# ScalarE splits off the high part of h, the last batch's routing moves behind a layer, SyncE asks for rows ahead of weights

## The reference

```python
def ffn(x, ...):                      # 8 experts, each token uses 2
    logits = einsum('bsd,de->bse', x, gate_w) + gate_b
    probs = softmax(logits, axis=1)   # over the 256 tokens of a batch
    vals, idx = top_k(probs, 2)
    h = relu(einsum('bsd,edo->ebso', x, w1) + b1)
    h = relu(einsum('ebso,eop->ebsp', h, w2) + b2)
    y = relu(einsum('ebso,eop->ebsp', h, w3) + b3)
    onehot = one_hot(idx, E)
    w_tok = einsum('bske,bsk->bse', onehot, vals)
    ind = onehot.max(axis=2)
    v = einsum('ebso,bse->eo', y, w_tok)
    return einsum('bse,eo->bso', ind, v)

# x (16, 256, 512), ctx (16, 256, 512), all f32; attention without a mask, scale 1/sqrt(512)
x = x + tanh(g_xattn) * softmax(layernorm(x) @ Wq @ K.T * scale) @ V     # K, V = ctx @ Wkv
x = x + tanh(g_ffn) * ffn(layernorm(x), ...)
```

## Time and profile before

| | us |
|---|---|
| median of 3 runs | 954.37 |
| the three runs | 958.21, 954.37, 951.24 |
| the profiled execution, its own time | 953.95 |
| its span in the profile | 952.2 |
| mean granted clock of TensorE | 0.981 |

### The profile page before, as it was taken

The page is one execution under the profiler, slowest core; times in us unless marked ns, Lnnn a source line. Parts: engine busy times, 40 slices in busy tenths (PEclk is TensorE's granted clock), DMA queues, the critical chain, the costliest instruction groups (busy, mean ns, idle before and its releaser), DMA issues.

```text
span 952.2 us, 18810 instructions
## 1 busy us (share of the span) xinstructions
PE 918.2 (96%) x5746; PEld 863.7 (91%) x5746; DVE 721.6 (76%) x1379; ACT 419.5 (44%) x594; POOL 454.7 (48%) x402
## 2 busy tenths in 40 slices
PE   9999999999999979999999999999999999999985
PEld 6989888899888869899999999999999999999981
DVE  5667787887888867876877786889877777777646
ACT  5454443544433455344444444444444444444311
POOL 4225444444434566653655453655544554455213
PEclk9999999999999998999999999999999999999995
DMA  6433322233211544446656777866565555564008
GB/s 233 155 114 110 130 91 88 93 127 115 106 66 67 143 128 84 135 90 184 184 165 172 208 215 221 239 222 184 133 173 158 150 154 148 150 185 119 17 16 352
DMA packets 91924, 138.67 MB, mean 146 GB/s; under 512 B 28528, under 2 KB 56944, under 8 KB 88688
## 3 DMA queue, kind: packets, MB, share of 16 engines
q1 hardware_dynamic: 84464, 120.86, 42.8%
q0 software_dynamic: 7424, 17.38, 6.2%
HBM read 106.66 MB, written 31.53 MB: 145 GB/s over the span
## 4 chain that ended last, share of the span: by engine, by line
PE 65%; issue 11%; POOL 7%; DVE 6%; DMA 5%; SPq 4%; ACT 1%; POOLq 0%; DVEq 0%; ACTq 0%
PE bank L1319 20%; PE bank L1320 19%; PE bank L1321 19%; POOL h_lo L674 4%; POOL xg L664 3%; DMA rows_dram<-xg 2%; DMA xg<-xn_dram,idx 2%; DVE x_all L1309 2%; PE bank L1333 1%; PE bank L1390 1%; SPq L541 1%; PE bank L1431 1%; DMA idx<-slot_pair 1%; SPq L463 1%; PE bank L1433 1%
## 5 line engine op out<-in xcount | busy, mean ns | idle before, releaser
L674 POOL TENSOR_TENSOR h_lo<-h,h_hi 128x704 fp32r<-128x704 f32 x96 | 183.6, 1916 | 245.2 <-DVE h_hi L1190 245.2
L1319 PE MATMUL bank<-h_hi,w_hi 128*128 128x352 f32 x752 | 245.7, 327 | 7.3 <-POOL h_lo L674 4.1
L1321 PE MATMUL bank<-h_hi,w_lo 128*128 128x352 f32 x752 | 243.6, 324 | 0.0
L1320 PE MATMUL bank<-h_lo,w_hi 128*128 128x352 f32 x752 | 242.6, 323 | 0.0
L930 DVE TENSOR_TENSOR w_lo<-w_raw,w_hi 128x2048 fp32r<-128x2048 f32 x72 | 181.0, 2514 | 22.4 <-ACT w_hi L825 18.0
L836 ACT ACTIVATE h<-bank,bias 128x352 f32<-128x352 f32 x192 | 95.8, 551 | 201.0 <-PE bank L1321 170.8
L825 ACT ACTIVATE w_hi<-w_raw 128x2048 fp32r<-128x2048 f32 x72 | 137.8, 1916 | 54.6 <-PE bank L1321 46.0
L1319 PEld LDWEIGHTS bank<-h_hi,w_hi 128*128 128x128 f32 x752 | 142.1, 189 | 9.6 <-issue 9.6
L1320 PEld LDWEIGHTS bank<-h_lo,w_hi 128*128 128x128 f32 x752 | 142.1, 189 | 0.0
L1321 PEld LDWEIGHTS bank<-h_hi,w_lo 128*128 128x128 f32 x752 | 141.7, 188 | 0.0
L1319 PE MATMUL bank<-et_hi,w_hi 128*128 128x352 f32 x384 | 125.0, 326 | 4.5 <-DVE part L1226 2.6
(11 more groups left out here) (202 smaller groups left out, 1767.1 us busy)
## 6 DMA issues: line engine op xcount, KB each, us to landing
w_raw<-in_w SPq DMA_DIRECT2D x24, 1024.0 KB, 5.1
xq<-rows_dram SPq DMA_DIRECT2D x80, 176.0 KB, 4.1
w_raw<-in_w SPq DMA_DIRECT2D x48, 256.0 KB, 6.1
rows_dram<-xg SPq DMA_DIRECT2D x20, 512.0 KB, 3.1
wb<-slot_pair SPq DMA_DIRECT2D x24, 352.0 KB, 4.1
xt_raw<-in_x_t SPq DMA_DIRECT2D x16, 512.0 KB, 3.9
c_raw<-in_ctx_t SPq DMA_DIRECT2D x16, 512.0 KB, 3.3
x_all<-in_x SPq DMA_DIRECT2D x16, 512.0 KB, 4.8
```

The costliest lines, as they stand in the source:

```text
L674: pool.tensor_tensor(h_lo[n][:, 2 * k:2 * k + 2], h[:, 2 * k:2 * k + 2], h_hi[n][:, 2 * k:2 * k + 2].bitcast(F32), ALU.subtract).then_inc( ...
L1319: pe.matmul(out_ap, lh, rh, start=(i == 0), stop=False)
L1320: pe.matmul(out_ap, lh, rl, start=False, stop=False)
L1321: last = pe.matmul(out_ap, ll, rh, start=False, stop=(i == n - 1))
```

## The change

- ScalarE makes `h_hi`, directly behind each half of the relu; `h_high` is gone from VectorE.
- TensorE transposes all three chunks of tile 0 in one go, `p_times_v` of the last batch comes ahead of the gate logits of batch 14, and the ranks of batch 13 go into the middle of the last `values`. ScalarE and VectorE split tile 0's first weights between the second and the third chunk.
- Layer 2 of tile 0 begins on the first half of `h` (`layer2_first`), and the last batch's rows are transposed between its output halves; `slots` of the last batch is awaited by tile 1's layer 2 and no longer by tile 0's layer 3. Banks are dealt out anew for this.
- SyncE issues in its loop: store of the rows, `idx`, quarters, weights of layer 1, bias, `wb`. VectorE's two small steps on `wb` and bias (`weights_of`) move ahead of the weights' subtraction. `early_table` moves behind `exp_bias` of batch 14.

The diff, cut:

```diff
@@ layer_banks, row_banks, gate_banks
-            first = {(0, 0): (0, 1, 2, 3), (0, 1): (4, 5, 6, 2), (1, 0): (2, 3, 0, 1)}
+            first = {(0, 0): (0, 1, 2, 3), (0, 1): (4, 5, 6, 0), (1, 0): (0, 1, 2, 3),
+                     (2, 0): (4, 5, 6, 0), (1, 1): (1, 2, 3, 7)}
...
-            first = {0: (1, 2, 0), 1: (4, 5, 6), 2: (3, 0, 1)}
+            first = {0: (1, 2, 0), 1: (4, 5, 6), 2: (1, 2, 3)}
...
-            return [bank[0], bank[1]] if isinstance(m, int) and m == B - 1 else bG
+            return [bank[4], bank[5]] if isinstance(m, int) and m == B - 1 else bG
@@ SyncE, tile
+                if has_tile(3, left) and not isinstance(j, int):
+                    store_rows(j + 3)
+                if has_tile(4, left):
+                    load_idx(j + 4)
                 if has_tile(3, left):
+                    if not isinstance(j, int):
+                        load_quarters(j + 3)
                     load_w(0, j + 3)
-                    if not isinstance(j, int):
-                        store_rows(j + 3)
                 if has_tile(1, left):
                     load_b(2, j + 1)
                     load_wb(j + 1)
-                if has_tile(3, left) and not isinstance(j, int):
-                    load_quarters(j + 3)
-                if has_tile(4, left):
-                    load_idx(j + 4)
@@ ScalarE, relu_half
                     act.activation(h[:, oc], layer_banks(n, m)[oc][:, 0:TILE], ACT.Relu,
                                    bias=bias[n][:, oc:oc + 1]).then_inc(relu_done[n], 1)
+                need(act, l_done[n + 1], 2 * m)
+                if n == 1 and isinstance(m, int) and m == 0:
+                    act.wait_ge(gate_done, B)
+                act.wait_ge(relu_done[n], DC * m + 2 * k + 2)
+                act.activation(h_hi[n][:, 2 * k:2 * k + 2], h[:, 2 * k:2 * k + 2], ACT.Copy).then_inc(h_his[n], 1)
@@ ScalarE, the change of phases
-            et_high(0)
+            et_high(0, range(2))
             split_w(0, 0)
+            et_high(0, range(2, TH))
             gate_exp(B - 2)
             split_w(1, 0)
             act.wait_ge(b_in[0], 16)
             relu_half(0, 0, 0)
+            relu_half(0, 0, 1)
             norm2(B - 1)
-            relu_half(0, 0, 1)
             et_high(1)
+            split_w(0, 1)
             gt_high(B - 1)
-            split_w(0, 1)
             split_w(2, 0)
             relu(1, 0)
+            split_w(1, 1)
             gate_exp(B - 1)
-            split_w(1, 1)
@@ VectorE, batch
+                if isinstance(b, int) and b == KNOWN + 2:
+                    early_table()
...
-                if isinstance(b, int) and b == KNOWN + 1:
-                    early_table()
@@ VectorE, the change of phases
-            et_low(0)
+            et_low(0, range(2))
             w_low(0, 0)
+            et_low(0, range(2, TH))
             gate_softmax(B - 2)
             attended(B - 1)
             w_low(1, 0)
-            h_high(0, 0)
             two_best(B - 2)
             et_low(1)
-            gt_low(B - 1)
             slots(B - 2, (B - 2) % 2)
             w_low(0, 1)
+            gt_low(B - 1)
+            w_low(2, 0)
             gate_softmax(B - 1)
-            h_high(1, 0)
-            w_low(2, 0)
+            w_low(1, 1)
             two_best(B - 1)
-            h_high(0, 1)
-            w_low(1, 1)
-            slots(B - 1, (B - 1) % 2)
             w_low(0, 2)
             et_low(2)
+            slots(B - 1, (B - 1) % 2)
+            weights_of(0)
             weighted_sum(0)
@@ TensorE
+            def values_with_ranks(m, c, ranked):
...
+                for i in range(DC):
+                    if i == DC // 2:
+                        ranks(ranked)
...
+            def layer2_first():
+
+                need(pe, w_los[1], 1)
+                for k in range(2):
+                    need(pe, h_los[0], k + 1)
+                    for oc in range(2):
...
+                        for i in range(2 * k, 2 * k + 2):
...
+                last.then_inc(l_done[1], 1)
...
                 if isinstance(m, int) and m == 1:
                     need(pe, relu_done[0], 2 * DC)
+                    if k == 1:
+                        need(pe, slot_step, NSTEP * (B - 1) + 4)
                 layer_half(1, m, k)
...
-                if isinstance(m, int) and m == 0 and k == 1:
-                    need(pe, slot_step, NSTEP * (B - 1) + 4)
@@ TensorE, the change of phases
-            ranks(B - 3)
-            values(B - 1, 1)
+            values_with_ranks(B - 1, 1, B - 3)
             pt_transposes(B - 1)
             xn2_transposes(B - 2)
             need(pe, qa_los, 2 * B)
-            row_transposes(0, range(2))
+            row_transposes(0)
+            p_times_v(B - 1)
             gate_logits(B - 2)
-            row_transposes(0, range(2, TH))
-            p_times_v(B - 1)
             layer1_half(0, 0)
             gate_transposes(B - 2)
             layer1_half(0, 1)
             row_transposes(1)
+            layer2_first()
+            ranks(B - 2)
             xn2_transposes(B - 1)
-            ranks(B - 2)
-            layer2_half(0, 0)
+            layer2_half(0, 1)
             gate_logits(B - 1)
-            layer2_half(0, 1)
             layer1_half(1, 0)
+            layer1_half(1, 1)
             gate_transposes(B - 1)
-            layer1_half(1, 1)
```

More of the change, by code:

```diff
@@ L1182, in w_low @@
                 low(w_lo[n][:], w_raw[n][:], w_hi[n][:], w_los[n])
-            def h_high(n, m):
-                need(dve, l_done[n + 1], 2 * m)
-                if n == 1 and isinstance(m, int) and m == 0:
-                    dve.wait_ge(gate_done, B)
-                for k in range(2):
-                    dve.wait_ge(relu_done[n], DC * m + 2 * k + 2)
-                    dve.tensor_copy(h_hi[n][:, 2 * k:2 * k + 2], h[:, 2 * k:2 * k + 2]).then_inc(h_his[n], 1)
             def transpose_blocks(m):
@@ L1196, in transpose_blocks, with et_low @@
                               xq[:].rearrange("p g (i k) -> p g k i", k=DC)).then_inc(et_ready, 1)
-            def et_low(m):
+            def et_low(m, chunks=range(TH)):
                 if not isinstance(m, int):
@@ L1280, in tile @@
                         transpose_blocks(j + 2)
+                weights_of(j)
+                if has_tile(2, left):
                     w_low(0, j + 2)
                     et_low(j + 2)
-                if has_tile(0, left):
-                    weighted_sum(j, last=(left == 1))
+                weighted_sum(j, last=(left == 1))
             tiles = tiles_in_use(dve)
@@ L1493, in layer1_half @@
                     need(pe, part_done, m - 1)
+                    if isinstance(m, int) and m == 2 and k == 1:
+                        need(pe, relu_done[1], 2 * DC)
                 layer_half(0, m, k)
+            def layer2_first():
[3 more added lines that the diff above has]
+                    for oc in range(2):
+                        z = layer_banks(1, 0)[oc][:, 0:TILE]
+                        rows = slice(oc * P, (oc + 1) * P)
+                        for i in range(2 * k, 2 * k + 2):
+                            pe.matmul(z, w_hi[1][:, i, rows], h_hi[0][:, i], start=(i == 0), stop=False)
+                            pe.matmul(z, w_hi[1][:, i, rows], h_lo[0][:, i], start=False, stop=False)
+                            last = pe.matmul(z, w_lo[1][:, i, rows], h_hi[0][:, i], start=False, stop=(i == DC - 1))
+                last.then_inc(l_done[1], 1)
             def layer2_half(m, k, left=AHEAD + 1):
```

29 lines of the change are left out of this document (16 added, 13 removed).

## The result

The changed kernel takes 945.66 us, median of 20 runs (942.43 to 954.11), against 955.08 (951.24 to 958.21, 20 runs) of the kernel before on the same chip: ratio 0.9907, 95% interval 0.9890 to 0.9924. The gain is 0.93%, with an interval from 0.76 to 1.10% that doesn't reach zero; it falls just short of the 1% that the forecast took as what a measurement can tell. The profiled execution took 942.43 us, span 940.3: it is the quickest of the 20.

What follows compares the result with a forecast made beforehand. TensorE, 96% busy, was taken as the bound, with about 34 us of idle time and low clock to win. Change of phases 6.7 plus loop 4.7 less 0.1 made 11.3 us: 943 us forecast, range 938 to 952.

Steps and rivals of the forecast that it cites:

- rival (b): Loop's waits stay, by the lock of w_lo against h_lo and full DMA queues; gain only 6.6, 947.8 us; chance 0.18.
- Start of tile 0: Change of phases: earlier transposes and w_lo let layer 1 of tile 0 begin 2.4 us earlier, bounds 0 and 3.4.
- Layer 2 of tile 0: Change of phases: layer 2 begins 6.3 us earlier, behind one wait of 2 to 3 us for h_lo.
- Routing put off: Start of tile 1: slots and et_low(2) no longer hold TensorE; waits of 1.07 and 0.83 go, 1.9 us.
- The clock: Change of phases: one new low-clock stretch behind the 2.7 us idle time costs 2.3 us, ends 0 and 2.6.
- rival (a): Change of phases: no low-clock stretch at all, loop as forecast; 2.3 us less, 940.7 us; chance 0.22.
- The term of the change of phases: Gain up to the start of tile 1, 9.0 less 2.3 for the clock: 6.7 us, ends 3 and 9.5.
- `h_hi` on ScalarE: Moving 96 copies off VectorE costs nothing, covered by TensorE's other layer; only the last tile loses 0.1 us.
- The loop: SyncE's earlier idx and fewer VectorE copies leave 2.0 of 6.7 us of waits: gain 4.7 us.
- (d): Loop: SyncE becomes the bound, late weights delay h_lo and stall TensorE in ten tiles; about 967 us; chance 0.06.
- (c): First tile by blocks, tile 4: gain partly given back, about 3 us waited at layer 1; 950 us; chance 0.12.
- (e): Reordering does not reach TensorE: norm2 behind relus and copies delays the chain as much; 953 us; chance 0.08.

Runs made afterwards that it cites:

- runs 1 to 8: Two groups: one or two parts of the change without the rest; changed kernel with SyncE's order wholly or partly put back, or without layer 2's halves; ratios 0.9906 to 1.0166.
- u_sp: Changed kernel with SyncE's loop order put back to that of the kernel before: 942.33 us, ratio 0.9906 to the kernel before.
- runs 9 to 12: Changed kernel again; and with SyncE's old order, plain, with 14 filler matmuls, or with w_low(1, 0) behind two_best(14); ratios 0.9868 to 0.9920.
- v_sp: Changed kernel with SyncE's old loop order, measured once more beside the changed kernel on one chip: 944.13 us, ratio 0.9891 to the kernel before.
- v_after: The changed kernel once more, unaltered, as yardstick on another group's chip: 945.72 us, ratio 0.9920 to the kernel before.
- v_swap: Changed kernel with SyncE's old order and VectorE's w_low(1, 0) put behind two_best(14): 942.14 us, ratio 0.9868 to the kernel before.
- p_hi: Kernel before with only h_hi moved to ScalarE, all other orders as before: 946.14 us, ratio 0.9946 to the kernel before.
- p_phase: Changed kernel with VectorE making h_hi and SyncE's old loop order, so only the reordered change of phases stays: 950.23 us, ratio 0.9984 to the kernel before.
- u_hi: Changed kernel with VectorE making h_hi again, SyncE's new order kept: 954.82 us, ratio 1.0043 to the kernel before.
- p_sp: Kernel before with only SyncE's new loop order, VectorE unchanged: 959.65 us, ratio 1.0087 to the kernel before.
- u_idxlast: Changed kernel with the indices issued last again; store, quarters, then weights stay in the new order: 966.80 us, ratio 1.0166 to the kernel before.

## Why the prediction was right, and where it was wrong

The sum was 11.3 us and the two profiled executions show 953.95 - 942.43 = 11.5; but the second is the quickest of its kernel, and the medians differ by 9.4, about midway between the forecast and rival (b) with its 6.6. The total is right in part by luck: the change of phases came as it was worked out, the loop's gain came by another way than the one given.

*Start of tile 0, -2.4.* Forecast 339.5; 338.9 to 339.6 in the six profiles on the chips of runs 1 to 8 (`u_sp` 339.04), but 341.02 in the one of the changed kernel and 340.75 to 341.62 in the four of runs 9 to 12. The worked chain holds in the six; what is lost in the five is about 2 us at 326 to 329 us, told of at the end. The remaining wait of 1.3 us is there (1.34), and with it the clock at 1.00.

*Layer 2 of tile 0, -6.3, one wait of 2 to 3 us for `h_lo`.* 353.06 behind 2.29 us, forecast 352; `u_sp` has 351.08. Right, down to the `rn` that waits for `w_lo`. *Routing put off.* No wait for `base`; 0.17 and 0.49 us at the logits and probabilities are what is left. Right.

*The clock, +2.3.* Counted as one new low stretch. It is there in nine of the ten profiles with the reordered change of phases that have the wait: the clock over 8 us behind it is 0.79 to 0.81 in `u_sp`, `v_sp`, `v_after` and `v_swap`, which wait 2.29 to 2.39 us, and 0.63 to 0.81 in the five that wait 3.19 to 4.81 us. The exception is the profiled execution of the changed kernel, 1.00 behind its 2.29 us. So rival (a) describes that execution and the forecast the usual one; that the 3.2 us between the quickest execution and the median come from this stretch fits in size and isn't shown. The term of the change of phases, 6.7 with ends 3 and 9.5, measured 7.6 there and 5.9 in `v_after`. The copies alone gave 1.5 (`p_hi` 412.49 for 413.96), the order alone 6.1 (`p_phase`) or 3.9 (`u_hi`) in profiles, and nothing clear of noise in the times of `p_phase`.

*`h_hi` on ScalarE, worth nothing: the step that failed.* The duration was right (0.794 us for an estimate of 0.83; 76.2 us in all; ScalarE 52%). The cover was right as well for the path over ScalarE: 7.7 us against 3.9, and no wait for `h_lo` in the loop of any kernel that takes it. What failed is that the same sum wasn't made for the path over VectorE that it replaces. The prediction compared copy with copy, 0.83 against 0.53 us, and left out what stands ahead of the copy there and what it does to GpSimd: 3.1 us behind `w_lo`, both halves of `h_lo` in a row at 5.60 us, 9.3 us from the relus to the complete `h_lo` in the loop's first round, where TensorE had 8.1 us to cover them with. With the copies gone from VectorE all four waits of the earlier trace rows go. The copies give 5.3 us of the loop, and `p_hi` alone 0.54%. The rows had hinted at it: 725 ns in the mean for a copy of 0.53 us, and 5.60 us for two `h_lo`, which the prediction put down to `w_lo` behind late quarters.

*The loop, gain 4.7, by SyncE's order above all.* 4.3 measured (1.9 in `v_after`), but not by this. The order costs 0.6 to 0.9% with the copies on VectorE and gives nothing with them on ScalarE. The prediction saw that `idx` comes earlier and missed that all else on SyncE, a queue in order, then stands behind the wait for the gather. The transpose of the first round waits 8.96 us for its quarters (6.94 in `u_sp` with the old order), where under 3 was to be the sign of this step. "Keeps the 1 MB out of the gather's way" was the wrong way round in the first round of the loop: there the weights went out 9.6 us later in `p_sp` and right ahead of the rows.

*Rivals.* (b) gave the waits of the loop to the lock between `w_lo` and `h_lo` and drew the wrong sum from it. The copy of `h` takes part in it too: 0.53 us by itself, 1.99 beside `h_lo`. The Trainium skill (SBUF — State Buffer, "Who interferes with whom") names casts among the instructions that can take the shared ports; the trace agrees, and by that rule the move of 96 copies is a gain in itself. (d) described the waits: 52.4 us for `w_raw`, single ones up to 5.8 us. The prediction had named long waits for `w_raw` as a sign that it is wrong, and they came without harm; as a sign it was no good. (Its own sum, 25 less 11.4 on 954.4, makes 968.) It didn't decide, because the stores are 24.4 us apart and `h_lo` was in time; in `u_idxlast` it did. (c) and (e) didn't come: 1.79 us at the first tile by blocks, and the reordering reached TensorE.

## What to carry to other kernels

A step that is short by itself but waits in an engine's queue costs its place in the queue, and no mean duration shows that: follow one late operand back, row by row, before calling a move free. In a queue that works in order, a transfer moved ahead brings its wait along, and whatever was moved behind it waits too; look for the circle from gather to store to indices and compare its round with the bound engine's. When a change has three parts, price each against the kernel without the other two: here one part was worth 0.5% alone, one cost 0.9% alone, and the cost of the second nearly vanished beside the first. The third moved the marks in its profile by 6 us and its median by 0.3 us: a profile is one execution, and a gain is read from the times.

## What the hardware did that I had not expected

GpSimd's operation on 128x2 elements, 0.20 to 0.24 us elsewhere, takes 2.03 to 2.09 us when it begins beside VectorE's subtraction of two SBUF tiles (2.26 us), and ends with it; in `v_swap` another operation of this size was caught in place of the first. A tiny instruction pays the whole rest of a large one.

At 326 to 329 us the changed kernel loses about 2 us, and so do all four profiles of runs 9 to 12, while none of the six kernels of runs 1 to 8 with this change of phases does. The loss goes with the chip that a group of runs had, or with something else that a group shares, and not with an edit: `u_sp` and `v_sp` are one kernel and fall on either side. In the changed kernel TensorE stands 0.61 us at 328.38 with nothing to wait for in the records, VectorE 2.35 us to 328.59, and ScalarE is busy 0.49 us at 325 to 330 us in place of 2.73 (`u_sp`), with the DMA engines full in both (share 1.07 and 1.08 at 325 to 330 us). What holds them up isn't in the records and wasn't tried; it stays open. The same wait of 2.29 us has a low clock behind it in three executions (`u_sp`, `v_sp`, `v_after`, 0.79 to 0.81) and none in another (the changed kernel, 1.00): for a wait of this length the low stretch was likely here and not certain.
